# Adapter and layer-0 weight loads of a four-layer kernel's prologue: eight 512-KB transfers, one 512-byte-row transfer, and a regroup on VectorE

## The reference, cut to what matters

```python
x = x + _L0_ffn_ref(_L0_cond_ref(x, cond_512, ...), L0_ffn_A, L0_ffn_B, L0_ffn_Wr, L0_ffn_br)
x = x + _L1_ffn_ref(_L1_cond_ref(x, cond_512, ...), L1_ffn_gate, L1_ffn_kernel, L1_ffn_bias,
                    L1_ffn_lora_A, L1_ffn_lora_B, L1_ffn_lora_A_shared, L1_ffn_lora_B_shared)
...
```

## Time and profile before

| what | value |
|---|---|
| median of 3 executions | 1854.97 us (1850.24 to 1859.41) |
| the profiled execution, its own time | 1860.89 us |
| its span in the profile | 1859.1 us |
| TensorE matmuls busy | 1749.3 us, 94% of the span |
| VectorE, ScalarE busy | 842.3 us (45%), 641.5 us (35%) |
| mean granted TensorE clock | 0.96 of full |
| DMA engines, mean busy share | 0.39 |

### The profile page before, as it was taken

How to read it: one execution, slowest core, us unless ns; L and a number is a source line. 1 busy time by engine, 2 the same in 40 slices (tenths; PEclk the granted TensorE clock), 3 DMA queues, 4 the chain that set the end, 5 groups by cost and what they waited for, 6 DMA issues and landing times.

```text
span 1859.1 us, 25964 instructions
## 1 busy us (share of the span) xinstructions
PE 1749.3 (94%) x9224; PEld 1452.1 (78%) x9224; DVE 842.3 (45%) x2338; ACT 641.5 (35%) x1198; POOL 58.1 (3%) x99
## 2 busy tenths in 40 slices
PE   5889999978999999999899999999998999999995
PEld 4768788767888888887788888888776888888873
DVE  5146655644334333456444444434554334334327
ACT  2346556433333233325333323322243333223310
POOL 2000000010000000011000000000002000000000
PEclk9789999968999999999999999999998999999995
DMA  6656678438232323325322222222142232322218
GB/s 125 134 113 159 161 167 187 114 76 124 72 84 80 78 78 90 82 58 145 87 78 77 55 77 56 77 65 66 37 114 63 79 88 76 79 75 78 76 46 337
DMA packets 227625, 181.76 MB, mean 98 GB/s; under 512 B 176184, under 2 KB 187672, under 8 KB 227294
## 3 DMA queue, kind: packets, MB, share of 16 engines
q1 hardware_dynamic: 222142, 173.35, 36.4%
q10 hardware_dynamic: 2640, 5.26, 1.0%
q0 software_dynamic: 2768, 2.13, 0.9%
HBM read 108.34 MB, written 42.99 MB: 81 GB/s over the span
## 4 chain that ended last, share of the span: by engine, by line
PE 51%; issue 22%; DVE 3%; ACT 1%; POOL 1%; DMA 0%; POOLq 0%
PE ps L1024 46%; PE ps L1158 2%; DVE w_lo L1498 1%; PE ps L1110 1%; DVE x_last L2025 1%; DMA raw<-in_L_ffn_W 0%; ACT w_hi L1494 0%; POOL limes_rep L1950 0%; PE ps L2082 0%; PE ps L2073 0%; PE ps L1101 0%; PE ps L1890 0%; ACT tail_hi L1657 0%; DVE tail_lo L1647 0%; DVE tail_lo L1498 0%
## 5 line engine op out<-in xcount | busy, mean ns | idle before, releaser
L1024 PE MATMUL ps<-xp_hi,filt 128*128 128x512 f32 x1024 | 330.9, 404 | 2.3 <-DVE tail_lo L1498 2.1
L1024 PE MATMUL ps<-w_hi,y_hi 128*128 128x512 f32 x768 | 308.2, 401 | 0.0
L1024 PE MATMUL ps<-w_hi,y_lo 128*128 128x512 f32 x768 | 304.5, 396 | 0.0
L1024 PE MATMUL ps<-w_lo,y_hi 128*128 128x512 f32 x768 | 304.0, 396 | 0.0
L1024 PEld LDWEIGHTS ps<-xp_hi,filt 128*128 128x128 f32 x1024 | 189.0, 191 | 43.4 <-DVE tail_lo L1498 2.3
L780 DVE SCALAR_TENSOR_TENSOR xp_lo<-ps,mods_pair,xp_hi 128x512 fp32r<-128x512 f32 x128 | 96.3, 752 | 267.7 <-ACT xp_hi L437 266.6
L437 ACT ACTIVATE xp_hi<-ps,mods_pair 128x512 fp32r<-128x512 f32 x128 | 88.2, 690 | 340.9 <-PE ps L1024 340.9
L1024 PE MATMUL ps<-xp_lo,filt 128*128 128x512 f32 x512 | 203.7, 398 | 0.0
L453 ACT ACTIVATE y_nat<-ps,mods_pair 128x512 f32<-128x512 f32 x128 | 99.6, 778 | 230.9 <-PE ps L1024 230.9
L1024 PEld LDWEIGHTS ps<-w_lo,y_hi 128*128 128x128 f32 x768 | 144.9, 189 | 34.8
L1024 PEld LDWEIGHTS ps<-w_hi,y_hi 128*128 128x128 f32 x768 | 145.0, 189 | 31.2
(11 more groups left out here) (327 smaller groups left out, 2877.4 us busy)
## 6 DMA issues: line engine op xcount, KB each, us to landing
x_in<-x_state SPq DMA_DIRECT2D x96, 256.0 KB, 3.9
x_res<-x_state SPq DMA_DIRECT2D x48, 512.0 KB, 4.0
x_state<-x_res SPq DMA_DIRECT2D x46, 512.0 KB, 2.9
filt<-filt SPq DMA_DIRECT2D x128, 128.0 KB, 2.7
filt<-filt SPq DMA_DIRECT2D x128, 96.0 KB, 2.4
raw<-in_x SPq DMA_DIRECT2D x16, 512.0 KB, 5.4
x_res<-in_x SPq DMA_DIRECT2D x16, 512.0 KB, 4.9
x_state<-raw SPq DMA_DIRECT2D x16, 512.0 KB, 3.9
```

The lines of the kernel that those rows point to most:

```text
L1024: ins = nc.tensor.matmul(out, st[x0], mv[x1], start=first and t == 0, stop=last and t == 2, **kw)
```

## The change

Layer 1's adapters come in eight transfers of 512 KB, each with 128 rows of 4 KB and a semaphore of its own, and TensorE's mixing step t waits for the t-th. Layer 0's B comes in one transfer of 512 KB whose pieces are 128 numbers (512 bytes: 8 successive outputs of one expert), so that partition p holds outputs 8p to 8p + 7. VectorE copies `nat_0` to the new tile `nat_s` (`regroup_0`), with the expert inside the output; transposed block t then holds output 8p + t at column p. The parts that ScalarE and VectorE copy out write these columns to the same even-odd order as before, with another pattern: runs of 256 with a step of 4 numbers in place of runs of 2. `SMALL_LOADS[0]` is 4.

```diff
+            nat_s = sb("nat_s", [P, 8, P], stack=area)
...
-                for ob in range(8):
-                    small(nat_0[:, ob].rearrange("p (h r) -> p h r", h=8),
-                          w(0, "ffn_B")[:, P * ob:P * ob + P, :].rearrange("h o r -> o h r"))
+                small(nat_0[:], w(0, "ffn_B").rearrange("h (p s) r -> p h (s r)", s=8))
...
-        SMALL_LOADS = (11, 3, 11, 7)
+        SMALL_LOADS = (4, 3, 11, 7)
...
+            if l == 0:
+                for half in range(2):
+                    hi, lo = (t[:, 0].rearrange("q (h p t) -> q t h p", h=2, t=4)[:, 2 * half:2 * half + 2] for t in (tail_hi, tail_lo))
+                    parts.append((hi, lo, ps[:, (7, 5)[half], :].rearrange("q (t h p) -> q t h p", t=2, h=2)))
...
+        def regroup_0(dve):
+
+            dve.wait_ge(s["small_loaded"], small_count(0))
+            nc.vector.tensor_copy(nat_s[:].rearrange("p s (h r) -> p s h r", h=8),
+                                  nat_0[:].rearrange("p h (s r) -> p s h r", s=8)).then_inc(s["nat_ready"], 1)
...
             pe.wait_ge(s["small_loaded"], small_count(0))
+            pe.wait_ge(s["nat_ready"], 1)
...
-            for ob in range(8):
-                last = tr(ps[:, (7, 5)[ob // 4], P * (ob % 4):P * (ob % 4) + P], nat_0[:, ob], ident[:])
+            for t in range(8):
+                last = tr(ps[:, (7, 5)[t // 4], P * (t % 4):P * (t % 4) + P], nat_s[:, t], ident[:])
...
-            sp.dma_start(mix_in[0][:], w(1, "ffn_lora_A").rearrange("n (c r) d -> c n (r d)", c=8)).then_inc(mix_loaded[0], 16)
-            sp.dma_start(mix_in[1][:], w(1, "ffn_lora_B").rearrange("n (c o) r -> c n (o r)", c=8)).then_inc(mix_loaded[1], 16)
+            for t in range(4):
+                sp.dma_start(mix_in[0][:, L * t:L * t + L], w(1, "ffn_lora_A").rearrange("n (c r) d -> r c n d", c=8)[t]) \
+                    .then_inc(mix_loaded[t], 16)
+            rows_b = w(1, "ffn_lora_B").rearrange("n (c t o) r -> t c n (o r)", c=8, t=4)
+            for t in range(4):
+                sp.dma_start(mix_in[1][:, L * t:L * t + L], rows_b[t]).then_inc(mix_loaded[4 + t], 16)
...
-            if t % 4 == 0:
-                pe.wait_ge(mix_loaded[t // 4], 16)
+            pe.wait_ge(mix_loaded[t], 16)
...
             dve_halves(dve, 0, 1, 1)
+            regroup_0(dve)
             dve_narrow_0(dve)
```

More of the change, by code:

```diff
@@ L229, in build @@
             small_loaded narrow_pe wide_pe raw_act raw_dve shared_ready bias_row kernel_loaded kernel_act kernel_dve
-            gate_loaded gate_ready mix_pe mix_act mix_stored mixed_loaded mixed_act mixed_dve base_act base_dve
+            gate_loaded gate_ready mix_pe mix_act mix_stored mixed_loaded mixed_act mixed_dve base_act base_dve nat_ready
             cleared sq_forms modw_T modw_out forms_hi
@@ L241, in build @@
         raw_loaded = [sem(f"raw_loaded{t}") for t in range(4)]
-        mix_loaded = [sem(f"mix_loaded_{m}") for m in "ab"]
+        mix_loaded = [sem(f"mix_loaded{t}") for t in range(8)]
         fin_loaded = [sem(f"fin_loaded{n}") for n in range(HELD)]
@@ L1467, in narrow_parts @@
                                   ps[:, WIDE_BANKS[b], 0:width * kn].rearrange("p (k w) -> p k w", w=width)))
-            if l in (0, 2):
-                for blk, rows in ((0, P),) if l == 0 else ((0, P), (1, 96)):
+            if l == 0:
+                for half in range(2):
+                    hi, lo = (t[:, 0].rearrange("q (h p t) -> q t h p", h=2, t=4)[:, 2 * half:2 * half + 2] for t in (tail_hi, tail_lo))
+                    parts.append((hi, lo, ps[:, (7, 5)[half], :].rearrange("q (t h p) -> q t h p", t=2, h=2)))
+            if l == 2:
+                for blk, rows in ((0, P), (1, 96)):
                     for half in range(2):
                         hi, lo = (natural(t[0:rows, blk])[:, 256 * half:256 * half + 256] for t in (tail_hi, tail_lo))
-                        bank = (7, 5)[half] if l == 0 else WIDE_BANKS[2 * blk + half]
+                        bank = WIDE_BANKS[2 * blk + half]
                         parts.append((hi, lo, ps[0:rows, bank, :].rearrange("p (m h) -> p m h", h=2)))
```

## The result

The changed kernel's median is 1849.34 us over 20 executions (1843.69 to 1855.66), beside 1856.1 us over 20 of the kernel before (1848.25 to 1862.89). The ratio is 0.9967 with an interval of 0.9954 to 0.9981, a gain of 6.1 us (3.5 to 8.5). 4.5 us were forecast, to 1850.5.

A forecast was written before the change was run, and what follows sets the result against it. TensorE's matmuls were taken to bound the kernel (busy 94%), transfers counting only where TensorE stands still; 3.4 us for the mixing stop plus 1.1 for the copies make 4.5, so 1854.97 becomes 1850.5 us, range 1844 to 1857.

The forecast's parts named there:

- What bounds the prologue: First 90 us: ScalarE's 9.23 us wait for the second pair of samples costs TensorE 3.4 us before mixing step 7.
- Minus 3.4 us: Mixing step 7: with the second pair of samples landed by 67.0, TensorE's stop goes, saving 3.4 us (73.52 - 70.14).
- Per byte I cost this at nothing: Adapter transfers: 4-KB rows cost no more per byte than 16-KB rows, so the adapters' 35.5 us become 35.5 to 38.
- The pair lands at 64.8 to 66.6: Second pair of samples: with B in 512-byte pieces it lands then, 65.5 taken, before the 67.0 needed to be hidden.
- Why is the pair late?: SP's queue: B's eight transfers hold SP for 51.76 us, so the second pair of samples is issued only at 62.41.
- minus 1.1: ScalarE's and VectorE's copies out of B before the first convolution: the new write pattern saves 1.1 us; other end, nothing.
- The regroup: VectorE's copy of `nat_0` before the transposes: 1.22 us, ended by 69.7 to 70.6, hidden, so costing 0.
- Eight or sixteen engines: Adapter transfers: slowest dimension stays 8, so the new rows don't widen the path; DMA share about half until 56 us.
- The clock gives more: Rival: TensorE's clock also gains from the closed stops, giving 1848.8 or 1840 us; chances 0.22 (small) and 0.08 (large).
- its small form: Clock rival: the fall to half level at 89.8 to 93.2 doesn't come, 3.4 us become 1.7: 1848.8; chance 0.22.
- Its large form: Clock rival: the clock rises already in the mixing, up to 8.9 us less than 1848.8: 1840; chance 0.08.
- Slower: Rival: the eight adapter transfers run one after another, 14 us more, the sum 1863 or up to 1873; chance 0.05.

The follow-up runs named there:

- e3: The changed kernel with SP issuing the second pair of samples only after TensorE's second pair's halves; 1855.43 us, ratio 1.0003 to the kernel before.
- e9: The kernel before, unedited, profiled once more; one execution, 1853.72 us.
- e4: The changed kernel again, unedited; 1849.84 us over 12 executions, ratio 0.9974 to the kernel before; its profiled execution took 1857.58 us.
- e1: The kernel before with only the eight adapter transfers, B and its copies as they were; 1849.46 us, ratio 0.9964 to the kernel before.
- e2: The changed kernel with the two old adapter transfers, so only B's part is new; 1856.56 us, ratio 1.0007.
- e11: The kernel with B's part alone (changed kernel, two old adapter transfers), profiled once more; one execution, 1853.97 us.
- e7: The changed kernel with B in 256-byte pieces, so that the copies out write with a step of 2 numbers; 1850.43 us, ratio 0.9962 to before.
- e10: The kernel before, unedited, profiled yet another time; one execution, 1853.91 us.
- e6: The changed kernel with the adapters in sixteen transfers by groups of 16 partitions, rows of 16 KB; one execution, 1848.8 us.
- e8: The changed kernel with B's copies and remainders writing whole runs of 512 without a step, reordering left out; one execution, 1846.74 us.

## Why the prediction was right or wrong

**What bounds the prologue: right.** The pair's wait was the price. With only the pair late, e3 is back at the time of before. That the forecast total lies inside the measured interval is partly luck: its 1.1 us for the copies came to nothing, its main term was too small, and the part of the change that was to bring the pair sooner was the wrong one.

**"Minus 3.4 us": the mechanism right, the size too small.** It was 73.52 - 70.14 in one profile, where "its earliest start is 70.14" was taken as a property of the kernel. It is one of that execution: full rate came at 52.3, and step 5 started at 63.22. With the adapters there early, step 5 starts at 57.5 to 58.2 in every profile with early full rate, and at 68.6 and 68.7 in the two with late. The kernel before got nothing from an early full rate (e9: 63.03), since step 4 waited for the second adapter transfer and the transposes for the pair. Means of the profiles: transposes at 77.7 before (three), at 72.0 with early adapters (six, of five kernels: 68.82, 80.01, 68.93, 69.12, 75.97, 69.29). That makes 5.7 us, and the medians say 6.1 (3.5 to 8.5). The interval holds the forecast's 4.5 too; that the true figure is above it is read from a few profiles, not shown by the times. The 12.1 us between the first two profiles were a matter of chance: the same change gives 3.3 between e4's profiled time and that of before.

**"Per byte I cost this at nothing": wrong, and this step failed.** The samples' 4-KB rows and the adapters' 16-KB rows had the same rate at full load in the earlier trace rows, but those were rates of mixtures. In eight transfers with 4-KB rows the adapters were through at 44.8 in place of 57.1, and at 39.7 with B left as it was (e1). It is the term put at nothing that carries the whole gain.

**"The pair lands at 64.8 to 66.6": wrong both ways.** It was worked out from B's short pieces. B alone leaves the pair at 68.7 (e2) and 68.8 (e11); the adapters alone bring it to 53.4 (e1). The answer to "Why is the pair late?" failed with it: SP was held nearly as long without B's eight issues (43.58 us at the router bias in e2, 51.76 before), and the pair, issued 8.7 us sooner, landed 1.7 sooner. It was late behind the adapters.

**The copies, "minus 1.1": wrong.** 2.05 and 2.04 against 2.08 and 2.07. The row taken as nearest had a step of 2 numbers, 8 bytes; the change's has 4, 16 bytes. The other end of the bound, "nothing", was the right one, and e7 measured what the row did stand for. The Trainium skill (SBUF — State Buffer, "Door 1: The DMA port swizzle") says that a line of 16 bytes wants two hits or more: at a step of 8 bytes a line gets two, at 16 one, and the trace agrees with that count (0.59 and 1.02 us). The Trainium skill adds there that 4 float32 can be strided for free; taken as a step of 4, the measurement speaks against it.

**The regroup: right that it is hidden.** It took 0.68 us in place of the 1.22 taken, and ended at 60.15; TensorE names no wait for it.

**Eight or sixteen engines: right** for the change's form. The half share was named for it; 0.73 came. That this is A, B and the pair passing in the same stretch is argued, not shown; e1, with B in its old form, has 0.74 over the same stretch.

**The rivals.** *The clock gives more*: its small form happened in part. There is no fall behind the stop before the first convolution, at full from 78.3 to 92.0, but it came then, and of the 12.1 us 2.6 lie behind the convolution. Whether this fall comes doesn't depend on the change. The same stretch in e9 and in e10, both the kernel before:

```profile
89.80:93.20 3.40, 3.40 (x17) 2.73 (x16) 0.17 (x1) 0.78 (x1) 0.00 (x0) 1.00 0.00 0
```

```profile
89.80:93.20 3.40, 3.40 (x10) 2.62 (x9) 0.00 (x0) 0.00 (x0) 0.00 (x0) 0.50 0.00 0
```

The kernel before goes without the fall once and has it twice (the earlier trace rows and e10), and e6, which has the early adapters, has it (0.51 from 81.1 to 84.6). Its large form, full rate carried through the mixing, didn't happen: steps 5 to 7 take 10.11.

*Slower*: refuted. The transfers of 512 KB overlap: they land 2.8 to 4.6 us apart where one of 2 MB takes 20.3, and e1 is faster than before. The Trainium skill (DMA: Bandwidth & Descriptors, "Rules for kernel authors") wants 1 MiB or more per transfer; here 512 KB with shorter rows beat both 1 MB and 2 MB, and the measurement decides. The Trainium skill (DMA: Bandwidth & Descriptors, "Anatomy of one DMA"), from which the prediction took 2.0 us, gives that figure for transfers issued from GpSimd; these leave through SP.

## What to carry to other kernels

A stop read from one profile is the distance between two paths in that execution: ask how far the other path moves from one execution to the next before taking the stop as the gain, above all where TensorE's rate sets it. Where one hardware queue feeds all, ask what is ahead in it, and not only what the issuing engine is held at: B's part alone brought the pair's issue 8.7 us forward and its landing 1.7. And when a row of another pattern gives a price, compare the step in bytes, not the word "step".

## What the hardware showed

Transfers with longer rows were slower: 98, 109 and 137 GB/s at 16, 8 and 4 KB on 8 engines each, and on all 16 the rows of 16 KB moved 169. Why, no run here tells; none changes the rows and leaves number and size of the transfers.

TensorE's first rise to full rate came at 39.9 to 41.9 us in seven of thirteen profiles, at 51.3 to 52.4 in four and at 62.9 and 63.3 in two; in the same kernel at 40.8 and at 62.9, with the matmuls in the same order. From 40.0 to 62.9 us in e4 TensorE stood still nowhere and stayed at half rate. The granted clock of the stretches can't be read for this. First one of e4, then one of the changed kernel's first profile:

```profile
40.00:62.90 22.90, 22.90 (x110) 22.14 (x108) 2.77 (x10) 6.48 (x8) 0.00 (x0) 1.00 0.42 76
```

```profile
40.80:57.80 17.00, 14.81 (x124) 14.32 (x124) 5.71 (x17) 8.80 (x13) 0.00 (x0) 1.00 0.71 145
```

Both say 1.00, but 110 matmuls took 22.90 us busy in the one and 124 took 14.81 in the other.

A mixing step of 3.68 and one of 1.89 stand to each other as the two levels, 1.2 and 2.4 GHz. What decides the moment stays open; it was not tried. So does a version that beats the change: e7, e8 and e6 are not to be told from it by their times.
